# Two per-rank expert lists instead of one, with results stored in list order and gathered back by node

## What is computed

```python
logits = tokens @ router_w.T                        # 3125 x 8
rw, re = top_k(softmax(logits), 2)
rw = rw / max(rw.sum(-1), 1e-12)
combine = zeros((N, 8)).at[arange(N)[:, None], re].set(rw)
out = tokens
for e in range(8):
    h = gelu(tokens @ w1[e] + b1[e])                # 256 x 256
    out = out + combine[:, e:e+1] * (h @ w2[e] + b2[e])
x = x + out                                         # tokens = layernorm(x)
```

## Time and profile before

| | us |
|---|---|
| three runs, median (lowest, highest) | 1933.62 (1933.04, 1933.66) |
| the profiled execution, its own time | 1931.48 |
| its span, from first to last instruction | 1929.7 |
| mean granted TensorE clock | 0.871 of full |
| busy over the span: PE, VectorE, ScalarE, GpSimd | 1421.6, 1219.7, 578.9, 1330.9 |
| routing, from the last gather of the layer before to the first expert gather | 1680.8 to 1743.3 |
| expert tiles, first gather to last result in `y_buf` | 1743.3 to 1877.6 |
| last scatter starts | 1887.0 |
| loads, combining and stores | 1889.5 to 1929.7 |

### The profile page before, as it was taken

The page is one execution under the profiler, slowest core; times in us unless marked ns, Lnnn a source line. Parts: engine busy times, 40 slices in busy tenths (PEclk is TensorE's granted clock), DMA queues, the critical chain, the costliest instruction groups (busy, mean ns, idle before and its releaser), DMA issues.

```text
span 1929.7 us, 22491 instructions
## 1 busy us (share of the span) xinstructions
PE 1421.6 (74%) x6268; PEld 932.5 (48%) x6268; DVE 1219.7 (63%) x2839; ACT 578.9 (30%) x1685; POOL 1330.9 (69%) x1333
## 2 busy tenths in 40 slices
PE   5666567769888887659999966676676777667970
PEld 3333255646555555537876433333333333366860
DVE  6999977789889887556424125454544444485544
ACT  0687511136566663133233311000000000053320
POOL 0688577777777777779886647777777777606771
PEclk9799779889999998879999989989867667658995
DMA  4011143445544443401102573333333333313338
GB/s 95 10 32 31 23 106 105 108 106 146 133 120 119 117 117 106 108 2 39 28 2 65 139 230 106 107 104 106 106 104 106 104 106 105 95 56 97 102 104 215
DMA packets 105430, 183.77 MB, mean 95 GB/s; under 512 B 31189, under 2 KB 69544, under 8 KB 105181
## 3 DMA queue, kind: packets, MB, share of 16 engines
q0 software_dynamic: 56384, 134.58, 26.7%
q1 hardware_dynamic: 47617, 45.20, 8.7%
q10 hardware_dynamic: 1308, 2.56, 0.5%
HBM read 151.60 MB, written 30.38 MB: 94 GB/s over the span
## 4 chain that ended last, share of the span: by engine, by line
POOL 33%; PE 25%; DVE 19%; issue 13%; DMA 8%; DVEq 1%; ACT 0%; SPq 0%; POOLq 0%; ACTq 0%
POOL gath L914 30%; DVE hot_c L655 6%; PE ps L955 6%; DMA gath<-y_tab,index_b 5%; PE ps L1397 4%; PE ps L1361 4%; PE ps L1346 3%; DVE hot_r L646 2%; PE ps L1786 2%; PE ps L1797 2%; DMA gath<-h_tab,index_a 2%; DVE gath L994 1%; DVE acc L946 1%; POOL slot_tab_b L742 1%; DMA wide<-y_nodes 1%
## 5 line engine op out<-in xcount | busy, mean ns | idle before, releaser
L955 PE MATMUL ps<-gath,hot 128*125 128x260 f32 (+1 forms) x1808 | 609.5, 472 | 287.8 <-DVE gath L994 103.2
L955 PEld LDWEIGHTS ps<-gath,hot 128*125 128x125 f32 x1808 | 352.4, 220 | 505.1 <-DMA gath<-y_tab,index_b 182.1
L914 POOL DMA_INDIRECT gath<-h_tab,index_a x464 | 445.8, 961 | 149.6 <-issue 136.5
L914 POOL DMA_INDIRECT gath<-y_tab,index_b x440 | 416.1, 946 | 166.8 <-issue 120.3
L946 DVE TENSOR_TENSOR acc<-acc,ps 125x257 f32 (+1 forms) x672 | 284.6, 424 | 319.0 <-PE ps L955 290.0
L687 PE MATMUL ps<-hot_c,pay 125*128 125x440 f16 (+1 forms) x901 | 194.1, 368 | 63.5 <-ACT pay L676 59.3
L742 POOL DMA_INDIRECT slot_tab_b<-sent_word_b,sent_to_b x136 | 168.5, 1239 | 36.3 <-issue 36.3
L732 POOL DMA_INDIRECT slot_tab<-sent_word,sent_to x102 | 130.2, 1277 | 82.6 <-DVE sent_to L494 51.8
L676 ACT ACTIVATE pay<-hot_r,plan_b 125x128 f16<-125x128 f16 x578 | 172.0, 386 | 0.0
L687 PEld LDWEIGHTS ps<-hot_c,pay 125*128 125x128 f16 x901 | 87.6, 101 | 161.9 <-ACT pay L676 81.2
L994 DVE TENSOR_TENSOR gath<-gath,ps 128x1024 f32<-128x1024 f32 x116 | 136.0, 1214 | 0.0
(11 more groups left out here) (366 smaller groups left out, 1895.4 us busy)
## 6 DMA issues: line engine op xcount, KB each, us to landing
y_tab<-ybuf SPq DMA_DIRECT2D x25, 448.0 KB
gath<-h_tab,index_a POOLq DMA_INDIRECT x464, 2.8
gath<-y_tab,index_b POOLq DMA_INDIRECT x440, 2.8
h_tab<-hbuf SPq DMA_DIRECT2D x25, 113.8 KB
...
```

The lines of the kernel that those rows point to most:

```text
L914: p.indirect_dma_start(gath[:, ring(k) + s, 0:width], None, table, bass.IndirectOffsetOnAxis(ap=index[g][:, col:col + 1], axis=0)).then_in ...
L955: ins = t.matmul(ps[0:NP, 4 + q % 2, 0:width], hot[:, s, :], gath[:, s, 0:width], start=(e == 0), stop=(e == n - 1))
```

## The change

There are two lists, of the nodes' first experts and of their second ones, each sorted by expert and padded by itself. `LIST` is 32 tiles, so `MOE_TILES` becomes 64. The first list is made first: its one-hots, its product and its `node_i` come ahead of the second list's row blocks on VectorE. The second list's `node_i` is worked out between expert tiles 3 and 4. The eight scans over tiles become one of 400 elements. Gathers go through 16 slots instead of 14.

The results are no longer scattered by node. SP stores each tile of `y_buf` (now eight buffers) in list order to `y_slots[0]` or `y_slots[1]` by a plain DMA of 128 rows. They come back by node with indirect gathers of 125 rows, one for each tile of nodes and list (`bring_back`): those of the first list into `acc`, two behind each expert gather from tile 48 on, those of the second list into `wide` after the last store has landed. VectorE adds the first list's rows for all 25 tiles and then the second list's tile by tile; SP stores each tile of the output as it is done, in DMAs of 112 and 13 rows.

```diff
 CHOICE = ((7, 24), (7, 17), (7, 10), (7, 3), (3, 0))
 
 CHOICE_AT = ((1, "up", 2), (1, "up", 6), (2, "up", 1), (2, "up", 4), (2, "up", 7), (2, "down", 1), (2, "down", 3), (3, "up", 2))
-MOE_TILES = (2 * N + EXP * 127) // 128
-MOE_BODY = 14
-MOE_HALF = MOE_BODY // 2
+
+LIST = (N + EXP * 127) // 128
+MOE_TILES = 2 * LIST
+MOE_BODY = 16
 MOE_TURNS = MOE_TILES // MOE_BODY
+Y_BODY = 8
 W1B = 2 * D + D + 2
-KTH = 32
...
-    y_nodes = nc.dram_tensor("y_nodes", [2 * N + MOE_TILES * 128, D], F32, kind="Internal").ap()
+    y_slots = [nc.dram_tensor(f"y_slots_{k}", [LIST * 128, D], F32, kind="Internal").ap() for k in range(2)]
...
-    y_buf = end.tile("y_buf", [128, MOE_BODY, D])
+    y_buf = end.tile("y_buf", [128, Y_BODY, D])
...
-    hot_er = gath[:, :, :].rearrange("p s c -> p (s c)")[0:NP, 0:NT * 128].bitcast(F16).rearrange("p (j r) -> p j r", r=128)
-    hot_ec = wide[0:NP, 0:2 * NT * MOE_TILES].bitcast(F16).rearrange("p (k t v c) -> p k t v c", k=2, v=2, c=MOE_TILES)
+
+    hot_er = [gath[:, lo:lo + GRP, :].rearrange("p s c -> p (s c)")[0:NP, 0:NT * 64].bitcast(F16).rearrange("p (j r) -> p j r", r=128)
+              for lo in (0, MOE_BODY)]
+    hot_ec = wide[0:NP, 0:2 * NT * LIST].bitcast(F16).rearrange("p (k t v c) -> p k t v c", k=2, v=2, c=LIST)
...
-                ins = t_eng.matmul(ps[:, 6, 0:2 * MOE_TILES], hot_er[:, k * NT + t, :], hot_ec[:, k, t, :, :].rearrange("p v c -> p (v c)"),
-                                   start=(k == 0 and t == 0), stop=(k == 1 and t == NT - 1))
-        ins.then_inc(nodes_made, 1)
+                ins = t_eng.matmul(list_p(k), hot_er[k][:, t, :], hot_ec[:, k, t, :, :].rearrange("p v c -> p (v c)"),
+                                   start=(t == 0), stop=(t == NT - 1))
+            ins.then_inc(nodes_made, 1)
...
+        v.tensor_tensor_scan(place[:, :, :, :].rearrange("p k e t -> p (k e t)"), sel[:, :, :, :].rearrange("p k e t -> p (k e t)"),
+                             zeros_e[0:NP, 0:2 * EXP * NT], zeros_e[0:NP, 0:1], ALU.add, ALU.add)
...
+        list_columns(v, 0)
+        list_rows(v, 0)
+        list_columns(v, 1)
...
+        list_nodes(v, 0)
+        list_rows(v, 1)
         v.tensor_scalar(sum_scale[:, :], rstd[:, :], 1.0, None, ALU.add)
         v.tensor_tensor(logit[:, :, :], logit[:, :, :], b8(rstd), ALU.mult).then_inc(logit_ready, 1)
...
+    def list_columns(v, k):
+        v.tensor_tensor(hot_ec[:, k, :, 1, :], iota_r[0:NP, 0:LIST].unsqueeze(1).to_broadcast([NP, NT, LIST]),
+                        spread(slot_col[:, k, :], LIST), ALU.is_equal).then_inc(er_col, 1)
+
+
+    def list_rows(v, k):
+        for t in range(NT):
+            ins = v.tensor_scalar(hot_er[k][:, t, :], iota_r[0:NP, :], slot_row[:, k, t:t + 1], float(t + 1), ALU.is_equal, ALU.mult)
+            if t % U5 == U5 - 1:
+                ins.then_inc(er_hot, 1)
...
+    def list_nodes(v, k):
+        v.wait_ge(nodes_made, k + 1)
+        rows, tiles = list_p(k)[:, 0:LIST], list_p(k)[:, LIST:2 * LIST]
...
+        v.scalar_tensor_tensor(node_i[:, k * LIST:(k + 1) * LIST], node_f[:, :], -float(NP + 1), away_e[:, :], ALU.add, ALU.max
+                               ).then_inc(moe_ready, 1)
...
-        for u in range(MOE_BODY):
+
+        def bring_back(k, t):
+            p.indirect_dma_start((acc_cols(t, D), flat(xb, t))[k], None, y_slots[k],
+                                 bass.IndirectOffsetOnAxis(ap=slot_i[:, k, t:t + 1], axis=0)
+                                 ).then_inc(second_back[t] if k else first_back, 16)
+
+        for u in range(MOE_TILES):
+            if u == LIST:
+                p.wait_ge(moe_ready, 2)
             gather_x(u)
-        p.wait_ge(moe_ready, 2)
+            lo = 2 * (u - LIST - MOE_BODY)
+            if lo == 0:
+                p.wait_ge(back_ready, 1)
+                for j in range(Y_BODY):
+                    p.wait_ge(y_put[j], 16 * (LIST // Y_BODY))
+            for t in range(max(lo, 0), min(lo + 2, NT)):
+                bring_back(0, t)
+        for j in range(Y_BODY):
+            p.wait_ge(y_put[j], 16 * (MOE_TILES // Y_BODY))
+        for t in range(NT):
+            bring_back(1, t)
+
+
+    def moe_sync(s):
         for u in range(MOE_TILES):
-            p.wait_ge(y_done, u + 1)
-            p.indirect_dma_start(y_nodes, bass.IndirectOffsetOnAxis(ap=dest_i[:, u:u + 1], axis=0),
-                                 y_buf[:, u % MOE_BODY, :], None).then_inc(y_put[u % MOE_BODY], 16)
-            if u + MOE_BODY < MOE_TILES:
-                gather_x(u + MOE_BODY)
+            s.wait_ge(y_done, u + 1)
+            s.dma_start(y_slots[u // LIST][u % LIST * 128:(u % LIST + 1) * 128, :], y_buf[:, u % Y_BODY, :]).then_inc(y_put[u % Y_BODY], 16)
...
+            if step == 4:
+                list_nodes(v, 1)
+            if step == 6:
+                v.tensor_copy(slot_i[:, :, :], slot[:, :, :]).then_inc(back_ready, 1)
...
-                if u >= MOE_BODY:
-                    v.wait_ge(y_put[u % MOE_BODY], 16 * (u // MOE_BODY))
+                if u >= Y_BODY:
+                    v.wait_ge(y_put[u % Y_BODY], 16 * (u // Y_BODY))
                 w1_at = at[u // MOE_BODY][u % MOE_BODY]
-                v.tensor_tensor(y_buf[:, u % MOE_BODY, :], ps[:, 4 + u % 2, 0:D], w1_flat[:, bass.ds(w1_at + 2 * D, D)], ALU.add).then_inc(y_done, 1)
+                v.tensor_tensor(y_buf[:, u % Y_BODY, :], ps[:, 4 + u % 2, 0:D], w1_flat[:, bass.ds(w1_at + 2 * D, D)], ALU.add).then_inc(y_done, 1)
 
...
-    def combine_loads(eng, sets):
-        y_rows = y_nodes[0:2 * N, :].rearrange("(t p k) d -> p t k d", p=NP, k=2)
-        eng.wait_ge(turned, MOE_TILES)
-        for u in range(MOE_BODY):
-            eng.wait_ge(y_put[u], 16 * MOE_TURNS)
-        for i in sets:
+    def combine_sync(s):
+        for t in range(NT):
+            s.wait_ge(combined, NT + t + 1)
             for lo, hi in SPANS:
-                eng.dma_start(set_rows[i][lo:hi], y_rows[lo:hi, i * U5:(i + 1) * U5, :, :]).then_inc(y_in[i], 16)
-
-    def combine_sync(s):
-        out_rows = out.rearrange("(t p) d -> p t d", p=NP)
-        s.wait_ge(nodes_made, 1)
-        combine_loads(s, (0, 2, 4))
-        for i in range(SETS):
-            tiles = slice(i * U5, (i + 1) * U5)
-            s.wait_ge(combined, 2 * U5 * (i + 1))
-            for lo, hi in SPANS:
-                s.dma_start(out_rows[lo:hi, tiles, :], xa[lo:hi, tiles, :]).then_inc(out_stored, 16)
-        s.wait_ge(out_stored, 16 * 2 * SETS)
+                s.dma_start(out[t * NP + lo:t * NP + hi, :], xa[lo:hi, t, :]).then_inc(out_stored, 16)
+        s.wait_ge(out_stored, 16 * 2 * NT)
 
     def combine_vector(v):
         v.wait_ge(x_added, 2 * NT)
+        v.wait_ge(first_back, 16 * NT)
         for t in range(NT):
-            i, u = t // U5, t % U5
-            v.wait_ge(y_in[i], 32)
-            for k in range(2):
-                if k:
-                    v.wait_ge(combined, 2 * t + 1)
-                v.scalar_tensor_tensor(flat(xa, t), set_rows[i][:, u, k, :], coef[:, k, t:t + 1], flat(xa, t), ALU.mult, ALU.add
-                                       ).then_inc(combined, 1)
-
-    def combine_scalar(a):
-        combine_loads(a, (1, 3))
+            v.scalar_tensor_tensor(flat(xa, t), acc_cols(t, D), coef[:, 0, t:t + 1], flat(xa, t), ALU.mult, ALU.add).then_inc(combined, 1)
+        v.wait_ge(combined, NT)
+        for t in range(NT):
+            v.wait_ge(second_back[t], 16 if t == RING else slot_filled(t, MOE_TURNS if t < MOE_BODY else 0))
+            v.scalar_tensor_tensor(flat(xa, t), flat(xb, t), coef[:, 1, t:t + 1], flat(xa, t), ALU.mult, ALU.add).then_inc(combined, 1)
```

More of the change, by code:

```diff
@@ L255, in build @@
     r_t = end.tile("r_t", [128, 2, EXP])
-    logit, prob, comb, sel, place, top, order = (
-        end.tile(n, [NP, NT, EXP]) for n in ("logit", "prob", "comb", "sel", "place", "top", "order"))
+    logit, prob, comb, top, order = (end.tile(n, [NP, NT, EXP]) for n in ("logit", "prob", "comb", "top", "order"))
+    sel, place = (end.tile(n, [NP, 2, EXP, NT]) for n in ("sel", "place"))
     s1, s2 = (end.tile(n, [NP, NT]) for n in ("s1", "s2"))
@@ L261, in build @@
     sum_scale = end.tile("sum_scale", [NP, NT])
[L262 to L267 removed]
+    node_f, held, place_f, away_e = (end.tile(n, [128, LIST]) for n in ("node_f", "held", "place_f", "away_e"))
+    node_i = end.tile("node_i", [128, MOE_TILES], I32)
+    cnt_e, sum_e, offs_e = (end.tile(n, [NP, 2 * EXP]) for n in ("cnt_e", "sum_e", "offs_e"))
+    tot_e = end.tile("tot_e", [EXP, 3, 2])
+    starts_e = end.tile("starts_e", [EXP, 2 * EXP])
     reach_e = end.tile("reach_e", [EXP, MOE_TILES])
+    slot_i = end.tile("slot_i", [NP, 2, NT], I32)
     tile_e = end.tile("tile_e", [1, MOE_TILES])
@@ L1570, in route_tensor @@
         t_eng.wait_ge(routed, 1)
-        t_eng.matmul(ps[0:EXP, 4, 0:1], cnt_e[:, :], ones[0:NP, 0:1], start=True, stop=True).then_inc(route_made, 1)
+        for k in range(2):
```

(30 more changed lines are left out.)

100 lines of the change are left out of this document (33 added, 67 removed).

## The result

| | before | changed |
|---|---|---|
| time, us, median of 5 runs | 1933.04 (1930.52 to 1933.66) | 1940.63 (1940.11 to 1943.51) |
| profiled execution, its span | 1929.7 | 1938.1 |
| first product of the tiles starts | 1747.81 | 1747.37 |
| last result (`y_buf`) starts | 1877.15 | 1884.72 |
| from there to the end of the span | 52.5 | 53.4 |

The ratio is 1.0045, 95% interval 1.003 to 1.0059. The forecast was 1931.7 and the range 1924.5 to 1938.0, so the time lies above the range.

The account below looks back on a forecast made before the run. GpSimd's bring-backs were taken to bound the end. 1745.9 + 124.6 + 9.2 + 0.9 + 3.6 = 1884.2 for the last result; stores and bring-backs end at 1927.8, 1.9 under 1929.7, so 1931.7; range 1924.5 to 1938.

Parts of the forecast that it names:

- first product: Start of TensorE's expert tiles: 4.54 us behind the first gather, at 1745.9 instead of 1747.8.
- register loads, three places: At tiles 16, 32 and 48 register loads hold up VectorE, then TensorE: 9.2 us in all, as before.
- waits for gathers, and the low clock behind them: Expert tiles: TensorE's earlier 8.2 us of waits for gathers are gone; none was put in the sum.
- second `node_i` and the rest of the tiles: Seven small VectorE steps before tile 4, 1.7 us, of which 0.9 come through to TensorE.
- last result to first bring-back: SP's last stores: 0.1 + 1.8 us after the last result, so GpSimd starts at 1886.1.
- 24 spacings of the bring-backs: The last 25 bring-backs set the end, 1.49 us apart: 24 x 1.49 = 35.8 us, to 1921.9.
- last start to landing: The last bring-back lands 3.0 us after its start: a gather's 2.75 plus 0.24 for the longer writing.
- addition, stores, end: After the last landing at 1924.9: one addition of 0.5 us, then the last pair of stores, end at 1927.8.
- Rival 3: Bring-backs that write longer still, beside SP's stores: slower by 3.9 us from 1.73 apart, 1941 at 1.8; chance 0.10.
- Rival 2: 125-row bring-backs go on five engines: spacing stays 1.49, the last lands 1.0 us later, 1932.7; chance 0.04.
- GpSimd's lead before tile 60: Three DMAs a step from gather 48, 4.23 us; gather 60 lands at 124.4, wanted at 128: cover holds by 3.5.
- The landing of `xn_tab`: The first gather waits for these stores: issued 1739.3, in 1.8 us later at 1741.1, bounds 1.3 and 3.4.

Follow-up runs that it names:

- e3: Changed kernel with the first list's additions made tile by tile, each just ahead of the tile's second one, instead of a run of 25: 1933.93 us, ratio 1.0015.
- e8: Changed kernel with the run of 25 first additions taking its second input from PSUM instead of SBUF: 1933.04 us, ratio 1.0006.
- m2: Kernel without the computation: streaks of 25 gathers beside various VectorE runs; longest gather 7.61 us beside additions as the kernel makes them, 1.37 beside tiny memsets.
- m1: Kernel without the computation: streaks of 25 indirect transfers by row count; a gather lasts 0.95 us with 128 rows, 1.20 with 125; landing 2.96 and 4.29.
- e1: Changed kernel with bring-backs of 128 rows instead of 125: 1926.27 us, ratio 0.9977.
- e2: Changed kernel with one bring-back of the first list behind each gather instead of two, the last nine before the last stores: 1931.83 us, ratio 1.0004.
- e4: Changed kernel with the small 13-row stores of `xn_tab` issued from ScalarE's queue instead of SP's: 1936.29 us, ratio 1.0027.

## Why the prediction was wrong

The profiled span was forecast at 1927.8 and is 1938.1, 10.3 us more.

| step of the prediction | forecast | measured | difference |
|---|---|---|---|
| first product | 1745.9 | 1747.37 | +1.5 |
| register loads, three places | 9.2 | 0.6 | -8.6 |
| waits for gathers, and the low clock behind them | 0 | 7.6 | +7.6 |
| second `node_i` and the rest of the tiles | | | +0.5 |
| last result to first bring-back | 1.9 | 3.15 | +1.2 |
| 24 spacings of the bring-backs | 35.8 | 42.06 | +6.3 |
| last start to landing | 3.0 | 4.9 | +1.9 |
| addition, stores, end | 2.9 | 2.8 | -0.1 |

- **The spacing failed, not by its price but by what stands beside it.** 1.49 was right within 0.02 (1.21 + 0.30 = 1.51). The step that let "the first list's rows" be "added before" asked only whether VectorE is in time. It did not ask what 25 instructions with two SBUF inputs do to GpSimd. 4.8 of the 6.3 us are the one long bring-back; the rest are several of 1.3 to 1.4. e3, e8 and m2 show it. Rival 3 named 1941 and a spacing of 1.8 (measured mean 1.75), but by bring-backs that are all longer; that mechanism did not occur.
- **"The trace's packets speak against" five engines was a false reading.** I took packets for engines. 125-row transfers of 1 KB leave 128 packets and still land late. Rival 2, with 0.04, was the right mechanism: it priced the landing 1.0 later, m1 shows 1.2 to 1.3, and with SP's stores beside it 1.9.
- **GpSimd's lead before tile 60.** The price of a step was right (4.23 forecast, 4.33 measured at 1864). The text says itself that the cover is gone if the register loads are cheap. They were, about 0.2 each. Gather 60 landed where the forecast had it, 124.4 us after the first product (1868.37 + 3.45 = 1871.82). But TensorE wanted it at about 118.6 and not at 128: 8.6 less for the register loads, and the rest because the transpose of tile 60 stands ahead of the product of tile 59, which the forecast left out. So 7.6 us took the place of the 8.6 saved, 6.0 of waits and the rest at the low clock (e1 and e2 each remove nearly all of it). The two had to be forecast as one: in this stretch only the later of TensorE and GpSimd counts. The cost of the loads was the term mis-sized most, 9.2 us for 0.6. Why they cost 3.1 on average before and 0.2 here, I did not find out.
- **The landing of `xn_tab`** does release the first gather, as forecast (e4). It landed 1.55 us after the last issue, within the bounds, but that issue came at 1740.06 and not 1739.3, GpSimd started 0.77 behind the landing and not 0.25, which was in no row, and its first gather took 1.41. The same restart, 0.82, stands behind the last store, where the sum had no term for it, and that store landed after 2.23 us and not 1.8.
- **Right:** the spacing of single bring-backs, the place of the first gather's wait, GpSimd as the bound of the end, and that the list chain of VectorE is not what starts the tiles.
